# Two attention layers with a long context: the context loads move from SyncE's DMA queue to ScalarE's

## The reference

```
q = ln(x);          x = x + attention(q, q)              # 16 heads of 8 channels
qc = ln(x);         x = x + attention(qc, ln(ctx))       # cross attention, first pass below
h = ln(x);          x = x + top2_of_8_experts(h)         # 128 -> 512 -> 128, gelu
```

## Time and profile before

| | us |
|---|---|
| median of 3 runs | 700.11 |
| lowest, highest | 699.45, 703.91 |
| the profiled execution | 697.61 |
| its span | 695.8 |
| PE busy | 557.6 (80%) |
| DVE busy | 428.1 (62%) |
| ACT busy | 327.3 (47%) |
| POOL busy | 151.1 (22%) |
| DMA queue 1 (all of the kernel's transfers) | 52.1% of 16 engines |

### The profile page before, as it was taken

One profiled execution on the slowest core, in us unless ns is written; L12 is line 12 of the kernel. 1 busy time (PEld: TensorE's weight loads), 2 busy tenths in 40 slices (PEclk: granted clock), 3 DMA queues, 4 the chain that ended last, 5 costly groups with the idle time before them and its releaser, 6 DMA issues.

```text
span 695.8 us, 16155 instructions
## 1 busy us (share of the span) xinstructions
PE 557.6 (80%) x6582; PEld 391.0 (56%) x6582; DVE 428.1 (62%) x1090; ACT 327.3 (47%) x495; POOL 151.1 (22%) x128
## 2 busy tenths in 40 slices
PE   1798745499979797999977949646998989889996
PEld 0677332265746565676745727333656657557674
DVE  5657567389868696977315201556786776767730
ACT  0265204156747473755642313213565665665563
POOL 1563112113131313220005000121130321303000
PEclk9899659589999998999987979867999999999998
DMA  4010946556748393865200761038869597696500
GB/s 153 18 45 14 128 94 88 90 83 97 118 63 127 64 126 60 106 79 70 91 1 3 137 114 60 1 72 113 104 109 145 75 139 117 81 152 76 70 4 14
DMA packets 25210, 57.44 MB, mean 83 GB/s; under 512 B 4532, under 2 KB 8748, under 8 KB 25140
## 3 DMA queue, kind: packets, MB, share of 16 engines
q1 hardware_dynamic: 25140, 56.45, 52.1%
HBM read 17.81 MB, written 0.23 MB: 26 GB/s over the span
## 4 chain that ended last, share of the span: by engine, by line
PE 29%; DMA 25%; issue 21%; DVE 12%; SPq 8%; POOL 2%; ACT 2%; DVEq 0%; ACTq 0%; POOLq 0%
DMA cx<-in_ctx 15%; DMA xT<-in_ctxT 7%; SPq L374 6%; DVE mxp L787 5%; PE SM L1165 5%; PE PO L1180 5%; PE MI L1096 4%; PE ST L1144 3%; PE MI L1120 2%; PE MI L1086 2%; DMA qall<-qsplit 1%; PE SM L1252 1%; DMA kst<-ksplit 1%; DVE qst L810 1%; DMA qst<-mrow 1%
## 5 line engine op out<-in xcount | busy, mean ns | idle before, releaser
L787 DVE TENSOR_REDUCE mxp<-SM 112x1 f32<-112x500 f32 x364 | 235.6, 672 | 77.5 <-PE SM L1165 76.5
L589 ACT ACTIVATE PT<-ST 128x896 f32<-128x896 f32 x192 | 171.6, 911 | 71.3 <-PE ST L1144 71.2
L1165 PE MATMUL SM<-kst,qst 96*112 96x500 bf16 x364 | 145.0, 412 | 48.4 <-DVE mxp L787 38.2
L1144 PEld LDWEIGHTS ST<-qst,kst 98*128 98x128 bf16 x1536 | 95.5, 101 | 38.0 <-issue 10.9
L1144 PE MATMUL ST<-qst,kst 98*128 98x112 bf16 x1536 | 109.8, 216 | 4.9 <-DMA qst<-mrow 4.8
L1180 PE MATMUL PO<-PT,vaug 125*32 125x112 f32 x3072 | 98.8, 267 | 3.0 <-ACT PT L589 1.5
L467 POOL TENSOR_TENSOR kr<-kf,ksplit 128x500 f32<-128x500 f32 x48 | 54.3, 1133 | 205.5 <-ACT ksplit L561 205.5
L1165 PEld LDWEIGHTS SM<-kst,qst 96*112 96x112 bf16 x364 | 47.3, 132 | 91.3 <-DVE mxp L787 70.6
L1180 PEld LDWEIGHTS PO<-PT,vaug 125*32 125x32 f32 x3072 | 72.0, 111 | 26.3 <-issue 16.8
L472 POOL TENSOR_TENSOR ksplit<-kr,ksplit 128x500 bf16<-128x500 f32 x48 | 54.5, 1136 | 79.3 <-DVE ksplit L782 79.3
L573 ACT ACTIVATE vaug<-MI 125x512 f32<-125x512 f32 x48 | 28.7, 598 | 85.3 <-PE MI L1096 85.3
(11 more groups left out here) (129 smaller groups left out, 572.2 us busy)
## 6 DMA issues: line engine op xcount, KB each, us to landing
kst<-ksplit SPq DMA_DIRECT2D x192, 187.5 KB, 7.7
cx<-in_ctx SPq DMA_DIRECT2D x8, 750.0 KB
xT<-in_ctxT SPq DMA_DIRECT2D x8, 750.0 KB, 8.2
moe<-in_w1T SPq DMA_DIRECT2D x8, 256.0 KB, 6.5
moe<-in_w2T SPq DMA_DIRECT2D x8, 256.0 KB, 7.5
qall<-qsplit SPq DMA_DIRECT2D x12, 112.0 KB, 5.4
watt<-in_watt SPq DMA_DIRECT2D x1, 768.0 KB, 5.6
qst<-mrow SPq DMA_DIRECT2D x32, 1.8 KB
```

What stands on the lines that cost most here:

```text
L589: nc.scalar.activation(PT[:, k % PTB], ST[:, k % 2, :, 0:4 * PC], ACT.Exp, scale=SCALE).then_inc(exp_done, 1)
L787: nc.vector.tensor_reduce(mxp[:, j // 3, j % 3:j % 3 + 1], tile_bank(j, banks), AX.X, ALU.max).then_inc(sm_red, 1)
L1144: last = mm(ST[:, k % 2, cc, PC * p:PC * (p + 1)], kst[n.par][:, 4 * half + p, at:at + 128], qst[n.par][:, 4 * half + p], start=True, stop ...
L1165: mm(tile_bank(j, banks), qst[n.par][0:SROWS, j // 3], kst[n.par][0:SROWS, j // 3, at:at + THIRD], start=True, stop=True).then_inc(sm_full, 1)
```

## The change

`load_ctx` and `load_xT` leave SyncE's list and enter ScalarE's, which has a DMA queue of its own. The places:

- `cx` of unit 2: at the end of turn 4 of the self-attention stage; of unit 3: behind the last turn; of units 4 to 7: at the head of windows 0 to 3 (that is unit `n+4` at the first step of window `n`);
- `xT` of units 3 to 7 of the second pass: in windows 0 to 4, behind the last third of the value projection's evacuation (step 6); of unit 2: in `start_pass(1)` behind the same evacuation; of units 0 and 1: in windows 5 and 6 of the first pass, step 6.

The waits are the same as before, on ScalarE now. `cx` of units 0 and 1 stay on SyncE.

```diff
@@ SyncE @@
             def load_ctx(n):
-                if n.it is not None or n.c >= 2:
-                    sp.wait_ge(xt_full, (n + -2).count(3, 3))
                 src = ctx_in[bass.ds(n.u, 1)].rearrange("a (p c) d -> (a p) c d", c=NCH)
                 sp.dma_start(cx[n.par][:], src).then_inc(ld_ctx[n.par], 16)
-
-            def load_xT(n):
-                sp.wait_ge(vp_full, (n + -2).count(3, 3))
-                src = ctxT_in[bass.ds(n.u, 1)].rearrange("a d t -> (a d) t")
-                sp.dma_start(xT[n.par][:], src).then_inc(ld_xT[n.par], 16)
...
             def window(n):
-                if n.s == 0 and (n + 3).exists():
-                    load_ctx(n + 3)
                 if (n + 1).exists():
                     restack(n + 1, 1)
                 shift(n, 1)
...
                     shift(n + 1, 0)
-                if n.s == 1 and (n + 3).exists():
-                    load_xT(n + 3)
...
-            load_ctx(Unit(0, None, 2))
...
-            load_xT(v0)
-            load_xT(v0 + 1)
...
-            load_xT(v0 + 2)
@@ ScalarE @@
+            def load_ctx(n):
+                act.wait_ge(xt_full, (n + -2).count(3, 3))
+                src = ctx_in[bass.ds(n.u, 1)].rearrange("a (p c) d -> (a p) c d", c=NCH)
+                act.dma_start(cx[n.par][:], src).then_inc(ld_ctx[n.par], 16)
+
+            def load_xT(n):
+                act.wait_ge(vp_full, (n + -2).count(3, 3))
+                src = ctxT_in[bass.ds(n.u, 1)].rearrange("a d t -> (a d) t")
+                act.dma_start(xT[n.par][:], src).then_inc(ld_xT[n.par], 16)
...
             def window(n):
                 own_mx, next_mx = n.mx_steps()
+                if n.s == 0 and (n + 4).exists():
+                    load_ctx(n + 4)
                 for k in range(STEPS):
...
                         evac_v(n + 1, k - V_STEP)
+                        if k - V_STEP == 2 and n.s == 1 and (n + 3).exists():
+                            load_xT(n + 3)
+                        if k - V_STEP == 2 and n.s == 0 and n.c + 1 >= B - 2:
+                            load_xT(Unit(1, None, n.c + 3 - B))
...
             def start_pass(s):
                 for i in range(3):
                     evac_v(first, i)
+                if s == 1:
+                    load_xT(first + 2)
...
                 if len(pieces) > 1:
                     evac_piece(*pieces[1])
+                if i == 4:
+                    load_ctx(u0 + 2)
+            load_ctx(u0 + 3)
             for i in range(3):
                 evac_k(u1, i, K_BANKS[i])
```

## The result

The changed kernel takes 723.82 us, the median of four runs (723.12 to 729.11), against 699.78 for the kernel before beside it. The ratio is 1.0366, with a 95% interval of 1.0303 to 1.0428. The forecast was 715 us in a range of 682 to 732. The direction, the mechanism in the main and the range held, and the size was 9 us too small; 2.2 of these lie in the base, as the sum starts from the profiled 697.61 and the median is 699.78. An execution in which the core's granted clock is low and the time over 1.5% above the fastest of the same kernel is left out of every median and ratio here: one of x1 (762.0 us, clock 0.711) and one of y4 (691.6).

The account below looks back on a forecast made before the run. Late `cx` and `xT` loads were taken to hold over a fifth of the chain, with no idle DMA bandwidth beside copies. The sum 697.6 + 8 + 0 - 8 + 17 + 0.5 gave 715 us, range 682 to 732.

Parts of the forecast that it names:

- What bounds the kernel: Whole kernel: late `cx` and `xT` loads hold 15% and 7% of the chain; no idle DMA bandwidth while copies fly.
- part 1: First pass, windows 0 to 4: all 27.5 us of DVE's waits for `cx` go, at most that much off the time.
- Part 2: Self-attention, end of turn 4: `cx` of unit 2 lands before DVE reads it; cost 0, up to 1 us.
- Part 3: Behind self-attention's last turn: `cx` of unit 3 delays SyncE's copies and `qall`; +8 us.
- Part 4, window 0: First pass, window 0: a PE wait for `kst` replaces DVE's 15.3 us wait for `cx`; net 0, bounds -12.4 to +1.5.
- Part 4, windows 1 to 3: First pass: PE waits 1.3 us for copies at tile 12, +4 in three windows; windows 1 to 4 together -8.
- Part 5: Five second-pass windows and first-pass window 5: `xT` makes copies and `qst` shift later, 2.8 us each; +17.
- Part 6: ScalarE: 14 added DMA issues may delay exponentials; +0.5 us, at most 11.
- Rival (a): Both passes: the loads fit into gaps and leave copies unharmed; 668 to about 680 us, chance 0.23.

Follow-up runs that it names:

- x1: The changed kernel run once more, unedited, for a second profile: 728.98 us, 1.0375 of the kernel before.
- y4: The changed kernel with ScalarE's window `cx` loads at step 4 instead of 0, unit 3's in `start_pass(0)`, and `xT` back on SyncE: 675.92 us, 0.9697.
- y1: The kernel before, all loads on SyncE, with `cx` of units 4 to 7 issued a window early behind the second half's copies and shift: 670.63 us, 0.9606.
- y2: The kernel before with each `cx` load cut into 112, 12 and 1 partitions, place and queue unchanged: 669.95 us, 0.9586.
- z3: The changed kernel with the small `qst` shifts also moved to ScalarE's queue, ahead of the loads: 714.02 us, 1.0187 of the kernel before.
- x2: The changed kernel with `xT` loads back on SyncE, so only the `cx` loads are on ScalarE: 713.68 us, 1.0187 of the kernel before.
- z4: As x3, with each `xT` load on ScalarE cut to 64 of 128 partitions: 711.08 us, 1.0142 of the kernel before.
- x4: The kernel before plus fourteen 256-byte DMAs issued by ScalarE at the moved loads' places, with their waits; loads stay on SyncE: 700.17 us, 1.0009.
- x3: The changed kernel with `cx` loads back on SyncE, so only the `xT` loads are on ScalarE: 713.78 us, 1.0176 of the kernel before.
- z2: The kernel before with `cx` placed as in y1 and cut as in y2, plus `qst` shifts issued on ScalarE's queue: 674.89 us, 0.9627.

## Why the prediction was right in direction and too small in size

**What bounds the kernel** and **part 1** held. All five DVE waits for `cx` are gone, and y1 shows what they were worth: 28.5 us came off when next to nothing took their place. That this is the 27.5 us of the waits is not the whole account: in windows 1 to 4 the waits of 12.2 us were worth 18 (y2), in window 0, where PE's own wait for `kst` stays, those of 15.3 were worth 12 (y1).

**Part 2**, `cx` of unit 2 at no cost: no engine waits for it. In the trace of the change self-attention ends 5.9 us later than before, and there TensorE's granted clock from 25 to 45 us was 0.52, against 0.83 before. The load does not explain it: it is issued at 52.9, behind that stretch, and y4 and z3 issue it at the same place and had 0.83; x2 had 0.66, x1 0.51, and z4, which keeps SyncE's load, 0.74. This is left open. It may be a part of what sets the profiled run above its median.

**Part 3**, +8 at the start: measured +8.4, `qall` waited for 12.4 us instead of 3.7. It landed at 110.5, not at 104, because everything stood 6 us later. The way there was in part another: only 4.8 us of it are the landing behind the last issue, 11.49 where the earlier trace rows have 6.73. About 4.0 are SyncE's own issues, which took up to 2.6 us each instead of 0.6; the sum had nothing for them.

```profile
98.98 11.49 DMA qall<-qsplit
```

**Part 4, window 0**, at nothing: measured +2.3, with a wait of 17.2 us for `kst` where about 15 were forecast. The 15.3 us freed were spent entirely.

**Part 4, windows 1 to 3**, is the step that was mis-sized. The forecast was a wait of 1.3 us a window and -8 for windows 1 to 4; the waits are 4.1 to 4.2, and the windows gave +1.3. The wait of 17.7 - 16.3, which is 1.4 and was taken as 1.3, became 4.1. Both of its numbers were off, and to the same effect. The half landed 19.5 us behind its first issue (193.77 - 174.29) instead of 17.7, since 16.1 and not 14.5 go by after the last issue. And PE came to tile 12 after 15.4 us (189.65 - 174.29) instead of 16.3. A difference of two numbers near 17 was carried with one decimal. Its upper bound of 4 us in each window was the truth. By the same numbers 2.3 of the 4.1 (17.7 - 15.4) would have come in one queue too, had only DVE's stall gone; the later landing adds 1.8.

**The clock** was not among the parts. Behind each 4.1 us wait PE ran at 0.50 for about 6 us: a window is 34.6 us against 27.8 without any wait, 4.1 of that the wait, and the remaining 2.7 I put to the clock. DVE's stalls before did much the same (0.82 in 230 to 238, windows of 33 to 34 us). So both terms of windows 1 to 4 were too small: against the 111.7 us of y2, which has neither, the waits removed were worth 18 and not 12, and the three new ones cost 19 and not 4. A stall of 4 us is worth 6 or 7 when it is truly removed.

**Part 5**, +17 for six windows at 2.8: measured +12.7 in the second pass, and +1.0 for window 5 and the experts. The cost of a window was a little larger, 3.2 to 3.5, but only three windows show it in full (541.10 to 635.03); the next has 1.7, and the one with the first load, issued at 517.12, is 28.2 us as before. `qst` waits of 2.9 to 3.4 us are what was forecast (3 to 5). The picture behind the number was in part wrong. `xT` does not share row by row with the copies, it starts late and then goes as a block ahead of the shift. PE's wait so grew by 2.2 to 2.4 us and the wait for `xT` (4.3 us in all before, 0.2 to 1.2 in a window, not 1.0 in each of five) went, which makes some 1.3 us net. The other 2 us I put to the stretch at 0.50 behind each wait, which no run isolates and the sum did not have. That 2.8 stood near 3.2 to 3.5 is luck, and so is the total, a cost too small times too many windows.

**Part 6**, +0.5: x4 has 1.0009 [0.9965, 1.0053], which can't tell 0.5 from nothing.

**Rivals.** Rival (a), the copies unharmed, would have been right if the loads had met no copies: y1 and y4 come near that case for `cx`, at 671 and 676, and the forecast had 668 to 680 for it. What spoke against it, a DMA share above 1.0 wherever a load was put, decided.

## What to carry to other kernels

With the engines already busy, the second queue here added no bandwidth: it took away the order in which the first one served its users, and some other transfer became late. Before moving a load to another queue, look in the DMA share for a stretch where little else flies, and put the load there. Here the `cx` loads moved within SyncE's list gave -4%, moved to ScalarE's queue beside the copies +1.9% (+3.7% with `xT`), and on that queue at step 4 of a window -3%. Also read share and GB/s of each load alone: a load at share 0.32 keeps a third of the engines busy, and cutting its partitions in 112, 12 and 1 gave the same 4% without moving anything.

## What the runs showed of the hardware

- A 750 KB load issued on ScalarE's queue beside copies of SyncE's queue behaved in two ways: `cx` (125 rows, share 0.32 when alone) alternated with the copies and took 14 to 21 us, `xT` (128 rows) went as a block of 4 us ahead of a shift that had been issued 0.1 us earlier (x3).
- The load's first row moved 4.9 us after its issue when five or six copies had been issued just ahead (`cx` at 76.18 in the change, `xT` at 561.12 in x3), and 0.9 to 2.2 us after it behind one or two.
- A DMA of 1.8 KB in a queue of its own moved up to 7.8 us after its issue beside the other queue's transfers (155.07 to 162.89), and 1.3 us with next to nothing beside it; PE waited up to 6.3 us for it (z2).
- A wait of 4.1 us on TensorE was followed by about 6 us at a granted clock of 0.50 (194 to 200 us) and full clock after that, in windows that otherwise run at 1.00. Waits of 3.1 to 3.4 us in the second pass were followed by 0.50 as well (586 to 592), where waits of 0.9 in the kernel before left it at 1.00.
- The same load of 768,000 bytes moved at 132 GB/s as one DMA of 125 partitions, alone in its stretch. As three of 112, 12 and 1 the stretch shows 242 GB/s, some rows of the slower on-chip copies among it.
- Half of `xT` (64 rows instead of 128) took 3.3 us in the mean from first to last packet, the whole 4.1 (z4, x3).
- Fourteen DMA issues with their waits on ScalarE, at 47% busy, cost nothing measurable.
